# Small attentions: one row maximum and one clamp for two units, where each unit had its own

## The chip, the cores and the metric

The kernel runs on one core of a Trainium2 chip. The metric is the device time of one execution in microseconds; where several executions are given, the median is meant. A core has TensorE (PE, matrix products and transposes), VectorE (DVE), ScalarE (ACT), GpSimd (POOL) and a queue that starts DMAs (SP). Each engine works through its own list of instructions strictly in the order in which the program wrote them; between engines, order comes from semaphores alone: an instruction waits until a counter has reached a value, and counts another one up when it ends.

## The reference

Thirty-two sequences of 128 tokens with 128 features (`x`) go through four layers, each a cross attention to a context of the same size and then a feed-forward part; every part reads a layer-normalised `x` and is added back to it with a gate `tanh(g)`. The parts differ: layer 0 is a 16-head attention with a mask and a mixture of experts, layer 1 a 16-head attention and an attention whose value and output projections are switched by a router, layer 2 an mLSTM and a convolution, layer 3 a one-head attention and another mixture of experts. What matters here are the two "small" attentions, those of layers 0 and 1:

```python
score = einsum('bhqd,bhkd->bhqk', qh, kh) / sqrt(8)      # 16 heads of 8 features, 128 x 128 scores each
score = where(mask == 0, -inf, score)                    # layer 0; layer 1: where(mask, score, -1e9)
attn  = softmax(score, axis=-1)                          # exp(score - max) / sum
out   = einsum('bhqk,bhkd->bhqd', attn, v) @ w_o + b_o
```

All arithmetic is in float32. The row maximum only keeps the exponentials in range; the clamp of layer 0 keeps a row that is masked throughout away from infinity.

## The kernel before, in words

**Tiling.** The 32 sequences are done in 8 turns. In a turn two lanes (`k` = 0 and 1) work side by side, each on G = 2 sequences, and each lane goes through the eight stages A0 (small attention of layer 0), M0, A1 (small attention of layer 1), SW, ML, CF, WA, M3. The lanes share the engines, and each lane has four of the eight PSUM banks: `banks[2k]` is one tensor of 1024 columns that covers its banks 0 and 1, `banks[2k+1]` its banks 2 and 3. `bank(k, n)` is one of them, 512 float32 columns.

**Order.** Every engine's work is written as a generator for each lane that yields between chunks. `weave` merges the two generators of an engine by tables of due times, `BEATS_PE`, `BEATS_ACT`, `BEATS_DVE`; the result is a fixed order of chunks, the same in every turn, in which chunks of lane 0 and lane 1 alternate. `SPARES` is a table of extra products of TensorE whose results nobody reads (L336). The change touches neither tables nor yields.

**A small attention** (`pe_small_attention`, `act_small_attention`, `dve_small_attention`) has 2 sequences x 16 heads = 32 score maps, in 8 units of 4 heads. Two units make a pair:

1. TensorE, `scores(p)`: for each of the pair's two units the mask is put into bank 0 (even unit) or bank 1 (odd unit), L383, and then the product of queries and keys is added to it, L386. The next pair's masks wait for `p_ok` of both units of this one.
2. VectorE, `dve_max` (L1202, called at L1238): the negated row maximum of the four maps of a unit, 128 x 512 in, 128 x 4 out, into the tile `nm`; in A0 a clamp of these four columns follows (L1206). Counts up `nm_ok`.
3. ScalarE, `act_map`: waits for `nm_ok` of its unit and makes four exponentials, L862, into `P`. Counts up `p_ok`.
4. TensorE, `pe_turn_map`: waits for `p_ok` of its unit and for the copy of the unit before, and makes four transposes into bank 2, L450.
5. VectorE copies them to `PT`, L1245 (`pT_ok`).
6. TensorE, `values(u)`: the product with the values, L397. After four units the outputs are turned (L408), and VectorE divides them by the row sums (`dve_small_out`, L1258 and L1260).

In VectorE's list of one lane the chunks are: maximum of the even unit, maximum of the odd unit, copy, copy, and again. Between the two maxima `weave` may put chunks of the other lane, and in each turn it does so for 10 of the 16 pairs. `dve_max` also serves SW and WA, which the change leaves as they are.

Of the kernel before, what the change touches and what calls it, by code (L numbers as in the profile page):

```python
# [11 lines left out]
ALU = mybir.AluOpType  # L12
ACT = mybir.ActivationFunctionType
AX = mybir.AxisListType
# [7 lines left out]
HQ = 4  # L22
NEG = -1.0e30
# [180 lines left out]
def b3(ap, n=G):  # L204
    return ap.rearrange("p (b c) -> p b c", b=n)
# [9 lines left out]
def cols(n, width=128):  # L215
    return slice(n * width, (n + 1) * width)


def build(nc, x_in, ctx_in, ctxT_in, mask0_in, mask1_in, w_in, pick_in, out):
    with ExitStack() as ctx:  # L220
# [3 lines left out]
        def pair(name, cols, dt=F32):  # L224
            return [sb(f"{name}_{k}", cols, dt) for k in range(LANES)]

        def sem(name):
            return ctx.enter_context(nc.semaphore(name))

        def signal(name, per):  # L230
            return Signal([sem(f"{name}_{k}") for k in range(LANES)], per)
# [10 lines left out]
        s_ps, nm_ok, p_ok = signal("s_ps", 25), signal("nm_ok", 25), signal("p_ok", 25)  # L242
# [16 lines left out]
        vt, at, = Ticks([sem(f"dve_step_{k}") for k in range(LANES)]), Ticks([sem(f"act_step_{k}") for k in range(LANES)])  # L259

        banks = [ctx.enter_context(nc.psum_tensor(f"banks{i}", [128, 1024], F32)) for i in range(4)]
# [42 lines left out]
        nm = pair("nm", 16)  # L304
# [15 lines left out]
        def bank(k, n):  # L320
            return banks[2 * k + n // 2][:, cols(n % 2, 512)]
# [781 lines left out]
        def dve_layernorm(dve, k, i, j, src, dst, sig):  # L1103
            s3, d3 = b3(src[:, :]), b3(dst[:, :])
            st3, mv3 = st[k][:, :].rearrange("p (b c) -> p b c", b=G), mv[k][:, :].rearrange("p (b c) -> p b c", c=2)
            for b in range(G):
                dve.bn_stats(st3[:, b, :], s3[:, b, :]).then_inc(vt.up(k), 1)
            dve.wait_ge(vt[k], vt.n[k])
            for b in range(G):
                dve.bn_aggr(mv3[:, b, :], st3[:, b, :]).then_inc(vt.up(k), 1)  # L1110
            yield from dve_rstd(dve, k, i, j, mv3[:, :, 1], 1.0, LN_EPS)
            dve.wait_ge(vt[k], vt.n[k])
            for b in range(G):
                e = dve.tensor_scalar(d3[:, b, :], s3[:, b, :], mv3[:, b, 0:1], mv3[:, b, 1:2], ALU.subtract, ALU.mult)  # L1114
            e.then_inc(sig, 1)
# [21 lines left out]
        def dve_gated_add(dve, k, i, stage, y, n):  # L1137
            dve.wait_ge(y_ps[k], y_ps.n(i, y))
            layer = stage // 2 + 4 * (stage % 2)
            dve.scalar_tensor_tensor(x[i % 2][k][:, :], bank(k, n)[:, 0:T], tg[:, layer:layer + 1], x[i % 2][k][:, :],  # L1140
                                     ALU.mult, ALU.add).then_inc(x_up[k], 1)
# [56 lines left out]
        def dve_max(dve, k, i, n, first, scores, maps, clamp):  # L1198

            m = nm[k][:, first:first + maps]  # L1200
            dve.wait_ge(s_ps[k], s_ps.n(i, n))
            e = dve.tensor_reduce(m, b3(scores[:, 0:maps * 128], maps), AX.X, ALU.max, negate=True)  # L1202
            if clamp:
                e.then_inc(vt.up(k), 1)
                dve.wait_ge(vt[k], vt.n[k])
                e = dve.tensor_scalar(m, m, -NEG / 10, None, ALU.min)  # L1206
            e.then_inc(nm_ok[k], 1)

        def dve_small_attention(dve, k, i, s):
            stage = (A0, A1)[s]  # L1210
            ln = dve_layernorm(dve, k, i, (VE_A0, VE_A1)[s], x[i % 2][k], xn[k], xn_ok[k])
            yield
            if s == 0:
                if i == 0 and k == 0:
                    dve.wait_ge(s_gates, 1)
                dve.wait_ge(x_ld[k], 16 * (i + 1))
                dve.wait_ge(ctx_ld[k], 48 * (i + 1))
                if i:
                    dve.wait_ge(x_up[k], x_up.n(i - 1, M3))
                dve.tensor_scalar(mb0[k][:, :], m_ld[k][:, :], 0.0, NEG, ALU.is_equal, ALU.mult)  # L1220
            else:
                dve.wait_ge(x_up[k], x_up.n(i, stage - 1))
            next(ln)
            v4 = va[k][:, 0:G * H * 32].rearrange("p (b h d) -> p b h d", b=G, h=H)
            if s == 0:
                dve.memset(va[k][:, 0:G * H * 32], 0.0).then_inc(vt.up(k), 1)
                dve.wait_ge(vt[k], vt.n[k])
                dve.memset(v4[:, :, :, DH], 1.0)
            yield
            dve.wait_ge(v_ps[k], v_ps.n(i, s))  # L1230
            dve.tensor_copy(v4[:, :, :, 0:DH].rearrange("p b h d -> p (b h) d"),
                            bank(k, 1)[:, 0:T].rearrange("p (n d) -> p n d", d=DH)).then_inc(v_ok[k], 1)
            yield
            next(ln, None)
            late = dve_constants(dve) if i + k + s == 0 else iter(())
            for u in range(8):
                yield
                dve_max(dve, k, i, 8 * s + u, 4 * (u % 4), bank(k, u % 2), HQ, s == 0)  # L1238
                if u % 2:
                    for n in (u - 1, u):  # L1240
                        yield
                        dve.wait_ge(pT_ps[k], pT_ps.n(i, 8 * s + n))
                        if n >= 2:
                            dve.wait_ge(o_ps[k], o_ps.n(i, 8 * s + n - 2))
                        dve.tensor_copy(PT[k][:, cols(n % 2, 512)], bank(k, 2)).then_inc(pT_ok[k], 1)  # L1245
                next(late, None)
            yield
            dve_small_out(dve, k, i, s, 0)
            yield
            dve_small_out(dve, k, i, s, 1)  # L1250
            yield
            dve_gated_add(dve, k, i, stage, (Y_A0, Y_A1)[s], 1)

        def dve_small_out(dve, k, i, s, b):
            rec = sm[k][:, cols(b, H)]
            o3 = bank(k, 2 * b).rearrange("p (h d) -> p h d", h=H)
            dve.wait_ge(ot_ps[k], ot_ps.n(i, 2 * s + b))
            dve.reciprocal(rec, o3[:, :, DH]).then_inc(vt.up(k), 1)  # L1258
            dve.wait_ge(vt[k], vt.n[k])
            dve.tensor_tensor(oa[k][:, cols(b)].rearrange("p (h d) -> p h d", h=H), o3[:, :, 0:DH], bc(rec, 2, DH),  # L1260
                              ALU.mult).then_inc(o_ok[k], 1)
# [393 lines left out]
        def dve_constants(dve):  # L1655

            part = mixd[0][:, 0:256].bitcast(BF16)
            rest = w("rows")
            dve.wait_ge(s_w1, 48)
            dve.tensor_copy(part, rest).then_inc(s_rows, 1)  # L1660
            dve.tensor_copy(causb[:, :], w("causal"))
            yield
            for m in range(3):
                pick = w("part3", m, m + 1)
                dve.wait_ge(s_rows, 3 * m + 1)
                if m == 0:
                    dve.tensor_scalar(rowsb[:, :], part, pick, None, ALU.mult).then_inc(s_rows, 1)
                else:
                    dve.scalar_tensor_tensor(rowsb[:, :], part, pick, rowsb[:, :], ALU.mult, ALU.add).then_inc(s_rows, 1)
                if m < 2:  # L1670
                    dve.wait_ge(s_rows, 3 * m + 2)
                    dve.tensor_tensor(rest, rest, part, ALU.subtract).then_inc(s_rows, 1)
                    yield
                    dve.wait_ge(s_rows, 3 * m + 3)
                    dve.tensor_copy(part, rest).then_inc(s_rows, 1)
            yield
            dve.tensor_copy(pick3b[:, :], pick_ld)
            dve.tensor_copy(pick0b[:, :], w("pick0"))
            yield
            dve.tensor_scalar(mb1[:, :], m1_ld[:, :], 0.0, NEG, ALU.is_equal, ALU.mult)  # L1680
            dve.tensor_scalar(bq1s[:, 0:1], w("bq1"), DH ** -0.5, None, ALU.mult)
            for j in range(HQ):
                e = dve.tensor_tensor(bkm[:, j:j + 1], w("bk1"), w("head4", j, j + 1), ALU.mult)
            e.then_inc(s_rows, 1)
# [247 lines left out]
```

## Time and profile before

| | |
|---|---|
| median of 3 runs | 2445.72 us (2435.81 to 2452.79) |
| profiled execution | 2447.47 us, span of its instructions 2445.4 us |
| TensorE busy | 2223.2 us (91%) |
| VectorE busy | 1749.4 us (72%), 5567 instructions |
| ScalarE busy | 1290.7 us (53%) |
| GpSimd busy | 141.2 us (6%) |
| mean granted TensorE clock | 0.976 |
| chain that ended last | TensorE 49%, VectorE 30%, ScalarE 8%, DMA 5%, issue 4% |

Busy is time in which an engine executes, idle is time in which it waits. Since every engine goes by its list, the idle time of one that is at work almost always (TensorE) is what a change can give or take. The chain is followed back from the last instruction; TensorE's share of it says that for about half of the span it was TensorE's own work that came last.

### The profile page before, as it was taken

Reading aid. Unit: us, or ns where it says so; the run is one execution under the profiler, and the core shown is the slowest. Engines: PE = TensorE matmul, PEld = TensorE weight load, DVE = VectorE, ACT = ScalarE, POOL = GpSimd, SP = SyncE. Lnnn points to the kernel's source line nnn. Section 1 sums busy time; section 2 is a strip of 40 time slices with the busy share of each in tenths; the row PEclk is TensorE's granted clock in tenths of the full one; section 3 lists DMA queues with packets and bytes.
Section 4 is the critical chain, followed back from the end, with each engine's and each line's share of the span. In section 5 each row is a group of like instructions: output and inputs, shape, how many; then the busy total and the mean of one; then the engine's idle time right before and its main releaser. Section 6 shows DMA issues by size and latency. Waiting matters only on the chain.

```text
span 2445.4 us, 51545 instructions
## 1 busy us (share of the span) xinstructions
PE 2223.2 (91%) x19938; PEld 1612.2 (66%) x19938; DVE 1749.4 (72%) x5567; ACT 1290.7 (53%) x3714; POOL 141.2 (6%) x180
## 2 busy tenths in 40 slices
PE   7899989989899998999899988999889998899998
PEld 3668657676567765677666766667666676666766
DVE  6874787757877577774877758777587775877657
ACT  4366354664547545474444744547344473445734
POOL 0000100001000010000100010000110001100010
PEclk9999999999999899998999999999899998999989
DMA  4034000340004300042000520006100061000610
GB/s 172 1 88 104 9 14 1 96 96 10 14 1 113 79 9 14 1 122 70 9 14 1 129 63 9 14 1 147 45 18 6 2 156 36 20 3 13 151 29 5
DMA packets 312516, 115.52 MB, mean 47 GB/s; under 512 B 268752, under 2 KB 295376, under 8 KB 312016
## 3 DMA queue, kind: packets, MB, share of 16 engines
q1 hardware_dynamic: 312272, 112.23, 17.9%
q8 instruction: 158, 2.59, 0.4%
q14 instruction: 86, 0.70, 0.1%
HBM read 63.96 MB, written 48.23 MB: 46 GB/s over the span
## 4 chain that ended last, share of the span: by engine, by line
PE 49%; DVE 30%; ACT 8%; DMA 5%; issue 4%; POOL 3%; SPq 1%; DVEq 0%; ACTq 0%
PE banks L450 7%; PE banks L386 6%; PE banks L589 3%; PE banks L505 3%; ACT PP L862 3%; PE banks L616 3%; PE banks L383 2%; PE banks L336 2%; DVE nm L1202 2%; DVE qk L1283 2%; DMA mix_d<-gs 2%; PE banks L544 2%; PE banks L397 2%; PE banks L559 2%; POOL mv L1741 2%
## 5 line engine op out<-in xcount | busy, mean ns | idle before, releaser
L862 ACT ACTIVATE PP<-banks,nm 128x128 f32<-128x128 f32 x1568 | 443.7, 391 | 210.8 <-DVE nm L1202 120.5
L1202 DVE TENSOR_REDUCE nm<-banks 128x4 f32<-128x512 f32 (+1 forms) x400 | 261.3, 675 | 136.3 <-PE banks L386 100.7
L336 PE MATMUL banks<-identb 128*128 128x256 bf16 x1840 | 289.1, 277 | 16.4 <-ACT PP L1017 8.5
L450 PE MATMUL banks<-w_sb,PP 128*128 128x128 f32 x1536 | 247.8, 285 | 45.7 <-ACT PP L862 17.6
L450 PEld LDWEIGHTS banks<-w_sb,PP 128*128 128x128 f32 x1536 | 167.4, 142 | 122.9 <-issue 64.0
L336 PEld LDWEIGHTS banks<-identb 128*128 128x128 bf16 x1840 | 177.2, 101 | 106.6 <-issue 48.0
L1741 POOL TENSOR_TENSOR mv<-mv,half 128x2 f32<-128x2 f32 x160 | 113.0, 706 | 2135.0 <-DVE mv L1099 2135.0
L1245 DVE COPY PP<-banks 128x512 f32<-128x512 f32 x256 | 175.8, 689 | 61.1 <-PE banks L450 60.2
L505 PE MATMUL banks<-w_sb,qk 128*128 128x128 f32 x1280 | 180.6, 280 | 2.0 <-DVE qk L1346 1.3
L505 PEld LDWEIGHTS banks<-w_sb,qk 128*128 128x128 f32 x1280 | 164.7, 194 | 20.1 <-issue 11.4
L386 PE MATMUL banks<-qk,gs 32*128 32x512 f32 x512 | 147.5, 653 | 0.0
L589 PE MATMUL banks<-va,PP 128*128 128x128 f32 x1024 | 139.3, 282 | 2.3 <-DVE oa L1391 2.3
L589 PEld LDWEIGHTS banks<-va,PP 128*128 128x128 f32 x1024 | 124.6, 194 | 8.5 <-DVE oa L1391 4.2
L853 ACT ACTIVATE xnT<-banks 128x256 f32<-128x256 f32 x128 | 49.1, 384 | 149.0 <-PE banks L344 149.0
L544 PE MATMUL banks<-xnT,w_sb 128*128 128x256 f32 x512 | 121.0, 384 | 0.6
L916 ACT ACTIVATE tmp<-banks 128x256 f32<-128x256 f32 x160 | 60.5, 383 | 103.1 <-PE banks L475 102.3
L544 PEld LDWEIGHTS banks<-xnT,w_sb 128*128 128x128 f32 x512 | 94.0, 190 | 25.4 <-issue 7.7
L397 PE MATMUL banks<-PP,va 128*32 128x128 f32 x2048 | 102.8, 284 | 3.9 <-DVE PP L1245 3.9
L1346 DVE TENSOR_TENSOR qk<-qk,banks 128x256 f32<-128x256 f32 x256 | 96.2, 416 | 8.2 <-PE banks L498 4.4
L1114 DVE TENSOR_SCALAR xn<-x,mv 128x128 f32<-128x128 f32 x256 | 76.7, 342 | 34.0 <-POOL mv L1741 32.6
L474 PE MATMUL banks<-xnT,w_sb 128*128 128x256 f32 x320 | 97.9, 388 | 0.5 <-DVE wstat L1700 0.5
L475 PE MATMUL banks<-xnT,w_sb 128*128 128x256 f32 x320 | 95.6, 381 | 0.0
(283 smaller groups left out, 4267.4 us busy)
## 6 DMA issues: line engine op xcount, KB each, us to landing
va<-v_d SPq DMA_DIRECT2D x32, 512.0 KB, 3.8
o_d<-oa SPq DMA_DIRECT2D x64, 256.0 KB, 4.2
va<-o_d SPq DMA_DIRECT2D x32, 512.0 KB, 4.4
pv_d<-PP SPq DMA_DIRECT2D x32, 256.0 KB, 2.0
oa<-pv_d SPq DMA_DIRECT2D x32, 256.0 KB, 3.2
v_d<-PP SPq DMA_DIRECT2D x16, 512.0 KB, 4.0
v_d<-tmp SPq DMA_DIRECT2D x16, 512.0 KB, 4.4
w_sb<-weights SPq DMA_DIRECT2D x1, 5599.0 KB, 24.2
```

Source lines behind the costliest of these rows:

```text
L336: pe.matmul(bank(k, n)[:, cols(c, T)], identb[:, :], bc(identb[:, :], 1, G), start=True, stop=True, skip_group_check=True)
L386: pe.matmul(bank(k, c), qT[k][rows, cols(b)], km[rows, b, :], start=False, stop=True, skip_group_check=True).then_inc(s_ps[k], 1)
L397: e = pe.matmul(bank(k, 3)[32 * j:32 * j + 32, cols(g)], v4[:, b, HQ * g + j, :], PT[k][:, 512 * (u % 2) + 128 * j:][:, 0:128], start=True ...
L450: e = pe.transpose(bank(k, 2)[:, cols(j)], P[k][:, 512 * (u % 2) + 128 * j:][:, 0:128], ident)
L474: pe.matmul(hb[:, 0:T], w("w1_0", n * 128, (n + 1) * 128), xnT[k][:, :], start=True, stop=True)
L505: e = pe.matmul(bank(k, 0)[:, cols(b)], qk[k][:, n * T + b * 128:n * T + (b + 1) * 128], w(weight, n * 128, (n + 1) * 128), start=n == 8 a ...
L544: pe.matmul(bank(k, n % 4)[:, 0:T], w(("sq1", "sk1")[n % 2], n // 2 * 128, (n // 2 + 1) * 128), xnT[k][:, :], start=True, stop=True).then_ ...
L589: e = pe.matmul(bank(k, 3)[:, cols(j)], PT[k][:, 512 * (u % 2) + 128 * j:][:, 0:128], va3[k][:, n:G * H + 1:G * H - n, :], start=True, sto ...
L862: e = act.activation(P[k][:, 512 * (u % 2) + 128 * j:][:, 0:128], bank_[:, cols(j)], ACT.Exp, bias=nm[k][:, m:m + 1])
L1202: e = dve.tensor_reduce(m, b3(scores[:, 0:maps * 128], maps), AX.X, ALU.max, negate=True)
L1245: dve.tensor_copy(PT[k][:, cols(n % 2, 512)], bank(k, 2)).then_inc(pT_ok[k], 1)
L1741: pool.tensor_tensor(a, a, half[:, 0:n], ALU.pow).then_inc(pw[k], 1)
```

## The change

`dve_small_attention` no longer calls `dve_max` for each unit. In the chunk of an even unit nothing is left; in the chunk of the odd unit `dve_max_pair` takes the maxima of both units in one instruction over both banks (128 x 1024 in, 128 x 8 out), clamps the eight columns once in A0, and counts `nm_ok` up by 2. Over the kernel 256 reductions of 512 columns become 128 of 1024, and 128 clamps become 64. ScalarE's and TensorE's waits keep their values, so the exponentials of an even unit now wait for the pair's instruction.

```diff
+        def dve_max_pair(dve, k, i, n, first, clamp):
+
+            m = nm[k][:, first:first + 2 * HQ]
+            dve.wait_ge(s_ps[k], s_ps.n(i, n))
+            e = dve.tensor_reduce(m, b3(banks[2 * k][:, :], 2 * HQ), AX.X, ALU.max, negate=True)
+            if clamp:
+                e.then_inc(vt.up(k), 1)
+                dve.wait_ge(vt[k], vt.n[k])
+                e = dve.tensor_scalar(m, m, -NEG / 10, None, ALU.min)
+            e.then_inc(nm_ok[k], 2)
+
...
             for u in range(8):
                 yield
-                dve_max(dve, k, i, 8 * s + u, 4 * (u % 4), bank(k, u % 2), HQ, s == 0)
                 if u % 2:
+                    dve_max_pair(dve, k, i, 8 * s + u, 4 * (u % 4) - 4, s == 0)
                     for n in (u - 1, u):
                         yield
                         dve.wait_ge(pT_ps[k], pT_ps.n(i, 8 * s + n))
```

## Rows read from the trace of the kernel before

**Rows 1.** Page, part 1: busy time, share of the span, instructions.

```profile
PE 2223.2 (91%) x19938; PEld 1612.2 (66%) x19938; DVE 1749.4 (72%) x5567; ACT 1290.7 (53%) x3714; POOL 141.2 (6%) x180
```

**Rows 2.** Groups of VectorE by form: count | busy us, mean ns | idle before, releasers.

```profile
L1202 DVE TENSOR_REDUCE nm<-banks 128x4 f32<-128x512 f32 x384 | 254.6, 686 | 136.3 <-PE banks L386 100.7 <-PE banks L559 34.1
...
L1206 DVE TENSOR_SCALAR nm<-nm 128x4 f32<-128x4 f32 x128 | 21.8, 170 | 4.4
...
L1202 DVE TENSOR_REDUCE nm<-banks 128x2 f32<-128x256 f32 x16 | 6.7, 418 | 0.0
```

**Rows 3.** Timeline of VectorE, A1 of turn 2: start us, length us, what [idle before].

```profile
723.39 0.69 DVE L1202 TENSOR_REDUCE nm<-banks 128x4 f32<-128x512 f32 x1 [0.54 <-PE banks L386]
724.00 0.68 DVE L1245 COPY PP<-banks 128x512 f32<-128x512 f32 x1
725.43 0.69 DVE L1245 COPY PP<-banks 128x512 f32<-128x512 f32 x1 [0.75 <-PE banks L450]
726.91 1.29 DVE L1202 TENSOR_REDUCE nm<-banks 128x4 f32<-128x512 f32 x2 [0.79 <-PE banks L386]
728.12 0.68 DVE L1245 COPY PP<-banks 128x512 f32<-128x512 f32 x1
...
732.71 0.68 DVE L1245 COPY PP<-banks 128x512 f32<-128x512 f32 x1
...
742.03 0.26 DVE L1258 RECIPROCAL sm<-banks 128x16 f32<-128x16 f32 x1
...
742.53 0.68 DVE L1202 TENSOR_REDUCE nm<-banks 128x4 f32<-128x512 f32 x1
```

**Rows 4.** Timeline of ScalarE, the same stage.

```profile
724.12 1.15 ACT L862 ACTIVATE PP<-banks,nm 128x128 f32<-128x128 f32 x4 [0.25 <-DVE nm L1202]
727.63 3.21 ACT L862 ACTIVATE PP<-banks,nm 128x128 f32<-128x128 f32 x12 [2.37 <-DVE nm L1202]
```

**Rows 5.** Timeline of TensorE, the same stage; the last rows from narrow windows.

```profile
718.81 0.63 PE L450 MATMUL banks<-w_sb,PP 128*128 128x128 f32 x4 [0.50 <-ACT PP L862]
...
722.23 1.13 PE L386 MATMUL banks<-qk,gs 32*128 32x512 f32 x4
723.29 0.66 PE L450 MATMUL banks<-w_sb,PP 128*128 128x128 f32 x4
...
726.81 0.66 PE L450 MATMUL banks<-w_sb,PP 128*128 128x128 f32 x4
...
728.92 0.63 PE L450 MATMUL banks<-w_sb,PP 128*128 128x128 f32 x4 [0.88 <-ACT PP L862]
...
734.44 0.66 PE L450 MATMUL banks<-w_sb,PP 128*128 128x128 f32 x4
...
743.27 0.63 PE L450 MATMUL banks<-w_sb,PP 128*128 128x128 f32 x4 [0.17 <-ACT PP L862]
```

**Rows 6.** Timeline of VectorE, A0 of turn 2.

```profile
633.99 0.69 DVE L1202 TENSOR_REDUCE nm<-banks 128x4 f32<-128x512 f32 x1 [1.06 <-PE banks L386]
...
649.91 0.68 DVE L1245 COPY PP<-banks 128x512 f32<-128x512 f32 x1
...
660.72 0.69 DVE L1245 COPY PP<-banks 128x512 f32<-128x512 f32 x1
```

**Rows 7.** Timeline of ScalarE, A0 of turn 2.

```profile
634.92 2.18 ACT L862 ACTIVATE PP<-banks,nm 128x128 f32<-128x128 f32 x8 [2.69 <-DVE nm L1206]
```

**Rows 8.** Timeline of TensorE, A0 of turn 2, in narrow windows.

```profile
651.32 0.30 PE L450 MATMUL banks<-w_sb,PP 128*128 128x128 f32 x1
...
662.41 0.66 PE L450 MATMUL banks<-w_sb,PP 128*128 128x128 f32 x4
...
668.40 0.63 PE L450 MATMUL banks<-w_sb,PP 128*128 128x128 f32 x4 [0.15 <-ACT PP L862]
```

**Rows 9.** Windows of two turns: length, busy of PE PEld DVE ACT POOL, granted clock, DMA.

```profile
1236.09:1534.80 298.71, 272.34 (x2493) 197.89 (x2493) 216.77 (x690) 161.07 (x464) 17.62 (x22) 0.99 0.18 44
1534.80:1838.07 303.27, 277.47 (x2494) 202.19 (x2493) 216.81 (x690) 161.16 (x464) 17.62 (x22) 0.97 0.18 44
```

## The prediction

> **What bounds the kernel now.** The page's first part comes first: TensorE is busy for 91% of the span, VectorE for 72%, ScalarE for 53% [rows 1]. So the time is TensorE's list of instructions plus the holes in it, and a change on VectorE counts only where it makes a hole of TensorE's wider or narrower. A turn of 298.71 us has 272.34 us of TensorE in it, so 26 us of holes [rows 9]. The timelines of one small attention on VectorE, ScalarE and TensorE tell which step ends a hole: TensorE stands before a unit's transposes (L450) for its exponentials, 0.50 us at 718.81, 0.88 us at 728.92, 0.17 us at 743.27 [rows 5], and the exponentials stand for the maximum [rows 4]. From the first maximum of a pair to the transposes of its even unit there is hardly slack in these places. That is where the change acts. The pattern is the same, to a few hundredths of a microsecond, in turns 1 to 7, and nearly so in A1 of turn 0; I work it out for turn 2.
>
> **What does not change.** All four products of a pair (two units) run as one group, 1.13 us from 722.23, to 723.36, and the even unit's maximum starts at 723.39 [rows 5, 3]. It does not start while the odd unit's products run, so waiting for both units costs nothing at this point.
>
> **The instruction itself.** 512 columns take 686 ns, 256 take 418 ns [rows 2]: 1.047 ns a column, so 1024 columns would take 686 + 512 x 1.047 = 1222 ns, an estimate from these two. Bounds: without any fixed part 1024 x 1.047 = 1.07 us; as two old ones, 1.37 us. I take 1.22, since the two forms are the same operation on the same memory. VectorE is relieved: in A1 by 2 x 0.686 - 1.22 = 0.15 us a pair, in A0, where one clamp of 0.170 goes too, by 0.32 us; with 64 pairs each 9.6 + 20.5 = 30 us of busy time. This is off the path except where TensorE waits for VectorE itself.
>
> **The even unit gets its maximum later.** Before, its exponentials start 0.73 us after the maximum starts (723.39 to 724.12), in A0 0.93 us (633.99 to 634.92), 0.20 us more for the clamp [rows 3, 4, 6, 7]. With the pair they start after 1.22 + 0.04 = 1.26 us, in A0 after 1.46 us. The exponentials take 1.14 us and the transposes follow 0.14 us later (727.63 + 1.15 + 0.14 = 728.92) [rows 4, 5]. So from the start of the pair's maximum to the transposes it is **2.54 us in A1, 2.74 us in A0**. The delay of 0.53 us is the small part.
>
> **The even unit loses its place in the queue.** The pair's instruction stands where the odd unit's stood. For 10 of the 16 pairs of a turn work of the other lane stands between the two, and the pair now waits for it. In A1 of lane 0 the even maximum runs at 723.39, then come two copies of lane 1 at 724.00 and 725.43, the second of which waits 0.75 us for TensorE, and only after lane 1's even maximum, in the middle of the row of two at 726.91, lane 0's odd one [rows 3]. In the new list lane 0 has no maximum before 725.43 + 0.61.
>
> Followed along TensorE's list through A1 (each later place starts from the shift reached so far):
> 1. Lane 0's second pair: its maximum starts about 716.90, its transposes at 719.44 instead of 718.81 [rows 5]: **+0.63**.
> 2. Lane 1's first pair: its products are 0.63 late, its maximum starts at 721.59, transposes 724.13 instead of 723.29: **+0.84**.
> 3. Lane 0's third pair: the copy at 725.43 goes to 726.27, the maximum follows after 0.61 us as at 723.39 to 724.00, so 726.88, transposes 729.42 instead of 726.81: **+2.61**.
> 4. Lane 1's second pair is behind lane 0's copy (728.12), and that copy now waits for the transposes just named: they end 0.66 us later, at 730.08, the copy starts at 730.11, the maximum at 730.72, transposes 733.26 instead of 728.92: **+4.34**. ScalarE's list has lane 1's exponentials of this unit ahead of lane 0's odd ones (the x12 of 727.63, three units), so lane 0's next transposes wait behind them as well.
> 5. Lane 0's fourth pair is behind lane 1's copy at 732.71, now 737.05; maximum 737.66, transposes 740.20 instead of 734.44: **+5.76**, of which TensorE's own small holes up to the next place give back 0.14.
> 6. Lane 1's last pair is behind the divisions of lane 0 at 742.03, now 747.65; its maximum follows after 0.50 us as at 742.53, so 748.15, transposes 750.69 instead of 743.27: **+7.4**.
>
> A0 in the same way, with 2.74 us and less VectorE time for the clamps:
> 1. The first pairs of both lanes add 0.6, and 0.2 come back where a copy no longer stands behind an even maximum; lane 1's units 0 and 1 bring it to 0.67.
> 2. Lane 0's third pair is behind lane 1's copy of 649.91, now 650.57; maximum 651.18, transposes 653.92 instead of 651.32: **+2.60**.
> 3. Two pairs add 0.24 (2.84). Lane 1's third pair is behind lane 0's copy of 660.72, now 663.56; maximum 664.17, transposes 666.91 instead of 662.41: **+4.50** [rows 6, 8].
> 4. Lane 1's last pair is behind lane 0's divisions as in A1, transposes some 674.6 instead of 668.40: **+6.2**.
>
> What is late next is everything: the last transposes stand in TensorE's list ahead of the output projection of lane 0, so the residual, the next layer norm and all later stages start with the shift. Nothing outside the attentions is loaded late enough by DMA to swallow it. Per turn 7.4 + 6.2 = 13.6 us, in 8 turns **109 us**.
>
> **The clock.** The list gets seven new holes a turn of 1.4 to 2.6 us. Turns at different granted clock differ in time for the same work: 298.71 us at 0.99, 303.27 us at 0.97 [rows 9], 4.6 us. Bounds for what the holes bring: 0, and one such step in each turn, 37 us. I take a quarter, 9 us, because a turn with 26 us of holes in it ran at 0.99 of the 2.4 GHz.
>
> **The sum.** 2447.5 (the profiled execution; 1.8 us above the median of the three runs) + 109 + 9 = **2565 us**, 4.9% slower.
>
> **Rivals.**
> - **A, VectorE's relief counts and the path hides the rest** (faster side). Place: the copies and maxima that TensorE waits for, and A0's clamps. Price: at most the 30 us above, 2417 us; half of it 2432. For it: the chain of waits gives 30% of the span to VectorE. Against it: TensorE's holes before transposes end with exponentials, not with VectorE. It decides if, in the places counted above, the transposes had 2 us of slack or more. The Trainium skill has a rule on this side, "VectorE: DVE Perf Modes", section "Rules for kernel authors": of chained VectorE operations, keep the number low. By that rule, the 192 instructions less would be a gain of up to these 30 us; the trace agrees on the busy time, but VectorE is not what fills the span. Chance 0.05.
> - **B, only the longer instruction counts** (place in the queue doesn't matter, as the other lane's work is ready early enough). Then a place costs 0.53 us; about 7 places a turn have no slack, so 3.7 us a turn, 30 us, 2477 us. For it: 6 pairs have nothing between. Against it: the copy at 725.43 itself waited for TensorE. Chance 0.09; with slack in half of these places 2462 us, within 1% of before, 0.05 more.
> - **C, the clock falls oftener**. One step from 0.99 to 0.97 in each turn and the whole shift: 2447.5 + 109 + 37 = 2593 us; two steps a turn 2630 us. For it: TensorE idles 2.6 us where it idled 0.88. Against it: turns with holes of their own at 0.99. The Trainium skill, "TensorE: Matmul & The Clock Gate", section "Part 1: The HAM clock gate", says that an idle TensorE goes to half rate, 1.2 GHz; by that, the seven holes are the risk. Chance 0.16.
> - **D, the change doesn't do what it says**: the reduction across two banks takes longer than 1.37 us, say 1.6. About 14 maxima of a turn are on the path; 0.38 x 14 x 8 = 43 us more, 2608 us. Nothing in the trace speaks for it. Chance 0.03.
>
> **The numbers.** The forecast, all of the shift with little clock, has 0.62. Its own range: 1.07 to 1.37 us for the maximum on 14 places in 8 turns is 17 us either way, the first turn's A0 (different work between) 6 us, and slips of the count some 20 us, so 2525 to 2600. The range over all reaches into C, **2515 to 2610 us**; outside are A, B and the far end of C and D. About 1% of the time, 24 us, is what a measurement can tell from no change. Faster by more: that part of A near its full price, 0.03. Within: the rest of A and the weak form of B, 0.07. Slower: 0.90.
>
> **What would show it.** VectorE's maxima: 128 of 128 x 1024 near 1.22 us, and VectorE's busy time down by some 30 us, in every case. For the forecast: TensorE's idle time up by about 110 us, nearly all of it before L450 and ended by L862; the third pair of lane 0 in A1 with its maximum some 2.7 us after its products instead of at once; turns of some 313 us; 7 us in A1 and 6 us in A0, and nothing in M0, ML, CF, WA, M3. For B: turns of 302 us. For C: a mean clock under 0.96. For A: turns under 298 us. I would be wrong if the transposes in the places above didn't move by the steps given, most of all steps 3 and 4 of A1.

## The result, and the profile after

The changed kernel takes 2633.64 us (median of 4 runs, 2626.35 to 2639.82), the kernel before 2445.97 us: the ratio is 1.0763 with a 95% interval of 1.073 to 1.0797. It is 188 us slower, where 2565 us, 119 us more, was forecast, in a range of 2515 to 2610 us. The sign was right; the time lies 24 us above the range.

The page of the changed kernel, first busy time and then the costliest groups that the change touches (line, engine, operation, form, count | busy us, mean ns | idle before, releaser):

```profile
PE 2324.9 (88%) x19938; PEld 1662.2 (63%) x19938; DVE 1729.1 (66%) x5375; ACT 1284.8 (49%) x3714; POOL 141.0 (5%) x180
...
L862 ACT ACTIVATE PP<-banks,nm 128x128 f32<-128x128 f32 x1568 | 440.0, 392 | 384.7 <-DVE nm L1217 181.1
L450 PE MATMUL banks<-w_sb,PP 128*128 128x128 f32 x1536 | 279.9, 311 | 138.9 <-ACT PP L862 116.2
...
L1213 DVE TENSOR_REDUCE nm<-banks 128x8 f32<-128x1024 f32 x128 | 155.5, 1217 | 49.9 <-PE banks L386 49.3
```

Against [rows 1] TensorE is busy for 102 us more, with the same 19938 products and transposes, and idle for 87 us more. So there are more holes, and the same work takes longer. Idle time before the transposes (L450) that the exponentials (L862) end is 116.2 us; in the trace of the kernel before it is 17.6 us. VectorE has 20 us less to do. The new maximum takes 1217 ns, against 1222 ns estimated from [rows 2].

The third and second pairs of A1, VectorE of the changed kernel, for [rows 3] (start us, length us):

```profile
778.18 0.69 DVE L1256 COPY PP<-banks 128x512 f32<-128x512 f32 x1 [0.75 <-PE banks L450]
778.79 1.21 DVE L1213 TENSOR_REDUCE nm<-banks 128x8 f32<-128x1024 f32 x1
781.99 0.69 DVE L1256 COPY PP<-banks 128x512 f32<-128x512 f32 x1 [1.99 <-PE banks L450]
782.60 1.21 DVE L1213 TENSOR_REDUCE nm<-banks 128x8 f32<-128x1024 f32 x1
```

ScalarE and TensorE of the same stretch, for [rows 4, 5]:

```profile
780.04 1.14 ACT L862 ACTIVATE PP<-banks,nm 128x128 f32<-128x128 f32 x4 [3.01 <-DVE nm L1213]
783.85 3.20 ACT L862 ACTIVATE PP<-banks,nm 128x128 f32<-128x128 f32 x12 [2.67 <-DVE nm L1213]
```

```profile
778.51 1.13 PE L386 MATMUL banks<-qk,gs 32*128 32x512 f32 x4
781.33 0.63 PE L450 MATMUL banks<-w_sb,PP 128*128 128x128 f32 x4 [1.69 <-ACT PP L862]
781.88 0.64 PE L397 MATMUL banks<-PP,va 128*32 128x128 f32 x16
785.13 1.09 PE L450 MATMUL banks<-w_sb,PP 128*128 128x128 f32 x4 [2.60 <-ACT PP L862]
...
788.64 2.08 PE L386 MATMUL banks<-qk,gs 32*128 32x512 f32 x4
...
792.54 2.08 PE L386 MATMUL banks<-qk,gs 32*128 32x512 f32 x4
```

This is to be seen: lane 0's maximum starts at 778.79 behind lane 1's copy, its transposes at 781.33, which is 2.54 us later. Those set lane 0's copy free (781.99), which lets lane 1's maximum start (782.60), and 2.53 us later lane 1's transposes run, at 785.13, after a hole of 2.60 us. The two holes of before were 0 and 0.88 us [rows 5]. Up to here it is the forecast step by step. But behind the hole the same instructions take twice as long: four transposes 1.09 us instead of 0.63, four score products 2.08 us instead of 1.13.

The granted clock of the two attentions of that turn and of the rest; then the stretches behind a hole in A0 and behind the hole of 2.60 us in A1 (length, busy of PE PEld DVE ACT POOL, clock, DMA):

```profile
668.00:726.00 58.00, 48.60 (x347) 27.51 (x345) 31.81 (x69) 24.47 (x82) 1.41 (x3) 0.85 0.04 11
726.00:766.00 40.00, 38.45 (x243) 32.14 (x243) 33.55 (x116) 14.10 (x41) 1.39 (x2) 1.00 0.00 1
766.00:812.00 46.00, 38.28 (x274) 19.61 (x273) 23.59 (x45) 19.95 (x68) 1.39 (x2) 0.81 0.00 1
812.00:967.00 155.00, 140.67 (x1484) 110.00 (x1482) 98.80 (x331) 85.66 (x230) 10.61 (x12) 0.96 0.32 76
```

```profile
693.30:706.90 13.60, 13.59 (x66) 6.01 (x66) 6.02 (x9) 4.90 (x19) 0.00 (x0) 0.54 0.01 1
785.13:798.80 13.67, 13.67 (x76) 6.58 (x76) 5.18 (x7) 6.32 (x25) 0.00 (x0) 0.53 0.00 0
```

And the kernel before with the same 66 products and transposes of A0:

```profile
651.32:659.43 8.11, 7.90 (x66) 3.73 (x66) 6.54 (x14) 5.89 (x21) 0.00 (x0) 1.00 0.01 2
```

TensorE works without a hole for 13.6 us at 0.54 of its clock (1.2 GHz in nearly all of it) for what before took 8.1 us at 2.4 GHz. That is 5.5 us in one turn's A0, and A1 has a stretch like it. Not every turn has both: in the changed kernel's trace A1 has one interval of 13.7 to 17.1 us at 1.2 GHz in turns 0, 2, 5 and 7, and of only 6.8 us in turns 1, 3, 4 and 6, with the same instructions in the same order.

"Half clock" below is time at 1.2 GHz. The profiled executions can be compared from the second turn on: there it is 92 us before and 324 us after. Over the whole spans it is 116 and 396 us, but the clock's record of the kernel before starts only 36.5 us into the span. The four score products take 2.08 us there, which is their length at half clock, and the changed kernel's trace has 24 us of half clock up to that time; about as much (an estimate) is missing in the 116:

```profile
24.64 2.08 PE L386 MATMUL banks<-qk,gs 32*128 32x512 f32 x4
```

The 117 us of the expectations below is that whole-span number.

### The profile page after: what moved, and what is told of

It is laid out like the page before. It is cut to its first block, busy times and chain, and to the rows that moved or that the text cites. A ratio compares the mean times of both kernels' runs of the same rounds, so it can differ in the third digit from the quotient of the medians.

```text
span 2634.1 us, 51481 instructions
## 1 busy us (share of the span) xinstructions
PE 2324.9 (88%) x19938; PEld 1662.2 (63%) x19938; DVE 1729.1 (66%) x5375; ACT 1284.8 (49%) x3714; POOL 141.0 (5%) x180
## 3 DMA queue, kind: packets, MB, share of 16 engines
q8 instruction: 158, 2.59, 0.4%
## 4 chain that ended last, share of the span: by engine, by line
PE 45%; DVE 31%; ACT 9%; DMA 5%; issue 5%; POOL 3%; SPq 1%; DVEq 0%; ACTq 0%
PE banks L450 8%; PE banks L386 5%; ACT PP L862 4%; DVE nm L1213 4%; PE banks L589 3%; PE banks L397 3%; PE banks L336 3%; PE banks L616 2%; DVE qk L1294 2%; DMA mix_d<-gs 2%; PE banks L383 2%; PE banks L505 2%; DVE tmp L1292 2%; POOL mv L1752 2%; PE banks L722 2%
## 5 line engine op out<-in xcount | busy, mean ns | idle before, releaser
L862 ACT ACTIVATE PP<-banks,nm 128x128 f32<-128x128 f32 x1568 | 440.0, 392 | 384.7 <-DVE nm L1217 181.1
L450 PE MATMUL banks<-w_sb,PP 128*128 128x128 f32 x1536 | 279.9, 311 | 138.9 <-ACT PP L862 116.2
L450 PEld LDWEIGHTS banks<-w_sb,PP 128*128 128x128 f32 x1536 | 186.4, 155 | 232.9 <-issue 166.5
L336 PE MATMUL banks<-identb 128*128 128x256 bf16 x1840 | 292.3, 279 | 13.6 <-ACT PP L1017 7.3
L1213 DVE TENSOR_REDUCE nm<-banks 128x8 f32<-128x1024 f32 x128 | 155.5, 1217 | 49.9 <-PE banks L386 49.3
L505 PEld LDWEIGHTS banks<-w_sb,qk 128*128 128x128 f32 x1280 | 168.9, 198 | 20.5 <-issue 11.4
L386 PE MATMUL banks<-qk,gs 32*128 32x512 f32 x512 | 169.3, 742 | 0.0
L397 PE MATMUL banks<-PP,va 128*32 128x128 f32 x2048 | 120.6, 327 | 1.6 <-DVE PP L1256 1.5
L544 PE MATMUL banks<-xnT,w_sb 128*128 128x256 f32 x512 | 120.9, 384 | 0.5
L1202 DVE TENSOR_REDUCE nm<-banks 128x4 f32<-128x512 f32 x144 | 89.6, 654 | 36.6 <-PE banks L559 36.3
L397 PEld LDWEIGHTS banks<-PP,va 128*32 128x32 f32 x2048 | 47.9, 120 | 86.0 <-issue 69.0
```

The source lines that it names most:

```text
L336: pe.matmul(bank(k, n)[:, cols(c, T)], identb[:, :], bc(identb[:, :], 1, G), start=True, stop=True, skip_group_check=True)
L386: pe.matmul(bank(k, c), qT[k][rows, cols(b)], km[rows, b, :], start=False, stop=True, skip_group_check=True).then_inc(s_ps[k], 1)
L397: e = pe.matmul(bank(k, 3)[32 * j:32 * j + 32, cols(g)], v4[:, b, HQ * g + j, :], PT[k][:, 512 * (u % 2) + 128 * j:][:, 0:128], start=True ...
L450: e = pe.transpose(bank(k, 2)[:, cols(j)], P[k][:, 512 * (u % 2) + 128 * j:][:, 0:128], ident)
L505: e = pe.matmul(bank(k, 0)[:, cols(b)], qk[k][:, n * T + b * 128:n * T + (b + 1) * 128], w(weight, n * 128, (n + 1) * 128), start=n == 8 a ...
L544: pe.matmul(bank(k, n % 4)[:, 0:T], w(("sq1", "sk1")[n % 2], n // 2 * 128, (n // 2 + 1) * 128), xnT[k][:, :], start=True, stop=True).then_ ...
```

## The experiments

The theories at this point: (1) the place in VectorE's list makes the shift, about 13.6 us a turn, and half clock that follows the holes makes the rest of the 188 us; (2) the longer instruction, or its read across two banks, makes the loss wherever it stands; (3) half clock costs nothing more, since it lies where TensorE waits anyway, and the list makes it all.

**The pair in the even unit's place.**

```diff
-                if u % 2:
-                    dve_max_pair(dve, k, i, 8 * s + u, 4 * (u % 4) - 4, s == 0)
+                if u % 2 == 0:
+                    dve_max_pair(dve, k, i, 8 * s + u + 1, 4 * (u % 4), s == 0)
+                if u % 2:
```

> The pair's maximum (one instruction over both banks, one clamp) stands where the even unit's stood, ahead of the other lane's work, and waits for the odd unit's products. Theory 1 (the place in VectorE's list makes the shift, 13.6 us a turn; the half clock that follows makes the rest of the 188 us): only the 0.53 us of the longer instruction are left, in some 7 places a turn, and some are given back by VectorE's relief: 2445 to 2480 us, mean clock 0.965 to 0.98, VectorE's maxima at 1.22 us as in the changed kernel. Theory 2 (the length of the instruction, or the read across two banks, makes the loss, wherever it stands): 2580 us or more, clock 0.93 to 0.95.

Measured: 2513.41 us, ratio 1.0287 (1.0225 to 1.0349), clock 0.965. Moving the instruction forward gives back 120 of the 188 us, so theory 2 is out. But it is 33 us above theory 1's range: the length is not as harmless as I had it. In the trace the waits of TensorE are longer by 0.1 to 0.67 us in some eighteen places, one after the other; the place of step 4:

```profile
749.51 0.65 PE L450 MATMUL banks<-w_sb,PP 128*128 128x128 f32 x4
750.10 0.64 PE L397 MATMUL banks<-PP,va 128*32 128x128 f32 x16
752.27 0.63 PE L450 MATMUL banks<-w_sb,PP 128*128 128x128 f32 x4 [1.53 <-ACT PP L862]
```

The hole is 1.53 us where it was 0.88 us before [rows 5]. Followed through turn 2, TensorE's list loses 3.8 us in A0 and 3.3 us in A1 against the kernel before, not 3.7 us in all. Little of it is the clock: half clock from the second turn on is 120 us, against 92 us.

**Two maxima in the odd unit's place** (the kernel before, edited).

```diff
-                dve_max(dve, k, i, 8 * s + u, 4 * (u % 4), bank(k, u % 2), HQ, s == 0)
                 if u % 2:
+                    for m in (u - 1, u):
+                        dve_max(dve, k, i, 8 * s + m, 4 * (m % 4), bank(k, m % 2), HQ, s == 0)
```

> Both units keep their own maximum and clamp of 512 columns, but the even one stands in the odd unit's place, just ahead of the odd one: the place alone, without the longer instruction. Theory 1: the even unit's exponentials start 0.53 us earlier than in the changed kernel on each of some 14 maxima of a turn that follow one another, so 13.6 - 14 x 0.53 = 6.2 us a turn and 50 us in all by the list, and half clock on top: 2500 to 2590 us, mean clock 0.94 to 0.97. Theory 2: as before the change, 2440 to 2455 us.

Measured: 2559.46 us, ratio 1.0441 (1.0401 to 1.0482), clock 0.945. The place alone, without any longer instruction, loses 111 us, as theory 1 has it; half clock from the second turn on is 208 us. Its holes are those of the changed kernel, each about half a microsecond shorter:

```profile
763.94 0.63 PE L450 MATMUL banks<-w_sb,PP 128*128 128x128 f32 x4 [1.16 <-ACT PP L862]
764.50 0.65 PE L397 MATMUL banks<-PP,va 128*32 128x128 f32 x16
767.21 0.63 PE L450 MATMUL banks<-w_sb,PP 128*128 128x128 f32 x4 [2.07 <-ACT PP L862]
```

1.16 and 2.07 us, against 1.69 and 2.60 us after the change.

**The changed kernel with its holes filled.** In front of seven waits of a turn TensorE gets products that nobody reads, into the bank that the transposes will overwrite.

```diff
+HOLES = {(0, 0, 4): 16, (0, 1, 4): 14, (0, 1, 6): 16, (8, 0, 4): 14, (8, 1, 2): 22, (8, 0, 6): 11, (8, 1, 6): 16}
...
             spare(pe, k, 2)
+            for _ in range(HOLES.get((first, k, u), 0)):
+                pe.matmul(bank(k, 2)[:, 0:T], identb[:, :], bc(identb[:, :], 1, G), start=True, stop=True,
+                          skip_group_check=True)
             pe.wait_ge(p_ok[k], p_ok.n(i, first + u))
```

> The changed kernel, with 11 to 22 extra products of TensorE that nobody reads (256 columns, 0.11 us each) put into the seven widest new holes of a turn, just ahead of the transposes that wait; the order of everything else and VectorE's work stay. Theory 1, by its two parts (109 us of shift by the list, some 80 us by half clock): the half clock goes and the shift stays, 2545 to 2580 us, mean clock 0.96 to 0.98. Rival (theory 3: half clock is only where TensorE waits anyway and costs nothing more, the list makes all 188 us): 2625 to 2645 us at a high clock.

Measured: 2553.5 us, ratio 1.043 (1.0398 to 1.0461), clock 0.97. This run separates the clock from the list: TensorE does 872 products more and the kernel is 80 us faster than the changed one. The same place as above, in its trace:

```profile
760.93 1.13 PE L388 MATMUL banks<-qk,gs 32*128 32x512 f32 x4
761.99 1.70 PE L451 MATMUL banks<-identb 128*128 128x256 bf16 x14
763.65 0.66 PE L455 MATMUL banks<-w_sb,PP 128*128 128x128 f32 x4
764.24 0.64 PE L399 MATMUL banks<-PP,va 128*32 128x128 f32 x16
764.82 2.58 PE L451 MATMUL banks<-identb 128*128 128x256 bf16 x22
767.40 0.66 PE L455 MATMUL banks<-w_sb,PP 128*128 128x128 f32 x4
```

The transposes come at the same distances as without the filling, 2.72 and 3.75 us apart, against 2.82 and 3.80 us; the shift stays. But both groups now take 0.66 us, at full clock, where the second took 1.09 us. Turn 2 as a whole (before, after, after with filled holes):

```profile
632.83:933.96 301.13, 275.99 (x2493) 200.06 (x2493) 216.92 (x691) 161.06 (x464) 17.62 (x22) 0.98 0.18 44
```

```profile
671.97:1001.42 329.45, 292.51 (x2493) 209.17 (x2493) 214.59 (x667) 160.43 (x464) 17.60 (x22) 0.92 0.17 40
```

```profile
660.62:973.03 312.41, 287.12 (x2602) 209.42 (x2601) 214.24 (x667) 160.66 (x464) 17.61 (x22) 0.98 0.17 42
```

301.1, 329.5 and 312.4 us. Over the five turns from the third on the mean length is 301.3 us before, 326.3 us after and 314.4 us with filled holes, so 13.1 us a turn are the list's, of which the forecast had 13.6, and 11.9 us are the clock's, of which it had 1.1. The clock is rightly called held: half clock in these five turns is 68 us before, 236 us after and 68 us with filled holes.

**The kernel before without its spare products** (`for _ in range(next(spares[k]))` becomes `range(0)`).

> The kernel before, without any of its spare products (L336); the order of the rest stays, and the maxima are those of before. It measures the price of the clock where VectorE's list is untouched. Theory 1: TensorE falls to half clock in the stages with small holes, half-clock time goes from 117 us to 250 us or more, and the time rises by some 0.3 us for each microsecond of it: 2480 to 2560 us, although 1840 products fewer run. Theory 3: the time stays or falls, 2420 to 2450 us.

Measured: 2511.96 us, ratio 1.0246 (1.0217 to 1.0275), clock 0.922. As theory 1 said: 1840 products fewer, nothing else changed, and 64 us more. From the second turn on the profiled execution is 51 us longer and has 287 us of half clock instead of 92 us, so 0.26 us for each microsecond of it. (From the kernel with filled holes to the changed one it is 79 us for 222 us, 0.36 us for each.) Theory 3 is out.

**Two maxima in the even unit's place.**

```diff
-                dve_max(dve, k, i, 8 * s + u, 4 * (u % 4), bank(k, u % 2), HQ, s == 0)
+                if u % 2 == 0:
+                    for m in (u, u + 1):
+                        dve_max(dve, k, i, 8 * s + m, 4 * (m % 4), bank(k, m % 2), HQ, s == 0)
```

> Both units keep their own maximum and clamp; both stand in the even unit's place. With the kernel before, the changed one and the two runs of a pair in the even place and of two maxima in the odd place it closes the table of place and length. Theory 1 (place and length each cost, each about what it adds from a pair's products to the transposes, and half clock follows the holes): the even unit loses nothing, the odd one comes earlier, only the other lane's copy is behind by 0.6 to 0.8 us where it stood between: 2435 to 2475 us, clock 0.97 to 0.98. Rival (two maxima in a row and the copies behind them hurt by themselves, wherever they stand): 2510 us or more, as the pair in the even place.

Measured: 2496.6 us, ratio 1.0205 (1.0181 to 1.0229), clock 0.96. It lies between both expectations, 22 us above theory 1's and 13 us below the rival's, so it is a miss for both. I had counted what a pair's own exponentials gain and not what the other lane loses. Now the copies of the other lane stand behind two maxima, and TensorE waits for them (two views of the same stretch, VectorE and TensorE):

```profile
658.67 0.69 DVE L1202 TENSOR_REDUCE nm<-banks 128x4 f32<-128x512 f32 x1 [0.79 <-PE banks L386]
659.40 0.17 DVE L1206 TENSOR_SCALAR nm<-nm 128x4 f32<-128x4 f32 x1
659.48 0.68 DVE L1202 TENSOR_REDUCE nm<-banks 128x4 f32<-128x512 f32 x1
660.19 0.17 DVE L1206 TENSOR_SCALAR nm<-nm 128x4 f32<-128x4 f32 x1
660.27 0.68 DVE L1247 COPY PP<-banks 128x512 f32<-128x512 f32 x1
```

```profile
661.01 1.09 PE L450 MATMUL banks<-w_sb,PP 128*128 128x128 f32 x8 [1.36 <-DVE PP L1247]
```

The hole of 1.36 us was 0.57 us before: the copy, next in line at 649.91 [rows 6], comes after 1.60 us here and came after 0.81 us there. The place matters to whoever stands behind, also where no instruction is longer and no VectorE work is added. In turn 2 TensorE's list loses 4 us up to the end of A1, of some 6 us a turn. Half clock from the second turn on is 143 us; where the rest of the loss arises was not followed.

**Two maxima in the odd place, holes filled.** Six holes, 9 to 18 products each, inserted as above.

> Two single maxima in the odd place as in the earlier run, with 9 to 18 extra products of TensorE that nobody reads in the six widest new holes of a turn. Theory 1: the shift by the list alone, 6.5 to 7.5 us a turn, stays and half clock goes: 2495 to 2520 us at a clock of 0.96 to 0.98, against 2559 us without them. Theory 3 (half clock costs nothing): 2550 to 2570 us.

Measured: 2507.92 us, ratio 1.0239 (1.0202 to 1.0276), clock 0.973; 52 us faster than without the filling. Half clock from the second turn on is 113 us instead of 208 us. Place alone at nearly held clock: 61 us, 7.6 us a turn.

**The kernel before with two of its own holes filled**: 17 spare products in front of the gates of M3 (lane 0), 12 in front of the first column sums of ML (lane 1).

> The kernel before with its own two widest holes filled in each turn: 17 unread products before the gates of M3 in lane 0 (hole of 2.31 us), 12 before the first column sums of ML in lane 1 (1.58 us). Theory 1 says that half clock costs 0.3 us for each of its microseconds: if the 117 us of half clock fall to 60 us or less, 2425 to 2440 us; if they stay, since what stands before and behind these holes is light work too, 2440 to 2455 us. Theory 3: 2440 to 2455 us in either case.

Measured: 2440.19 us (10 runs), ratio 0.998 (0.9965 to 0.9995), clock 0.98. It is the only version that is not slower than before, and by 0.2% only. From the second turn on half clock is 58 instead of 92 us. At the 0.3 us of theory 1 these 34 us would be worth 10 us; the measured gain is 7 us, with an interval of 1 to 9 us. That is too small a step to tell the theories apart, and the price may be lower here.

**A pair only where nothing stands between** (6 of 16 pairs of a turn; VectorE's order is that of before).

```diff
+                if (s, k, u // 2) not in ((0, 0, 0), (0, 0, 1), (0, 1, 1), (1, 0, 0), (1, 0, 1), (1, 1, 0)):
                     dve_max(dve, k, i, 8 * s + u, 4 * (u % 4), bank(k, u % 2), HQ, s == 0)
+                elif u % 2:
+                    dve_max_pair(dve, k, i, 8 * s + u, 4 * (u % 4) - 4, s == 0)
                 if u % 2:
-                    dve_max_pair(dve, k, i, 8 * s + u, 4 * (u % 4) - 4, s == 0)
```

> One maximum for two units only in the 6 of 16 pairs of a turn where no work of the other lane stands between the two, so VectorE's order is that of before; the other 10 pairs keep two maxima. The length alone, where the place is no question. Theory 1: 0.5 to 0.65 us in the places without slack, 4 or 5 of the 6: 2.0 to 3.2 us a turn, 2460 to 2475 us, clock 0.965 to 0.975. Rival A of the prediction (relief of VectorE counts): 2430 to 2445 us.

Measured: 2470.5 us, ratio 1.0098 (1.0068 to 1.0128), clock 0.976. The length alone, with the clock nearly where it was (half clock from the second turn on 96 us, against 92): 24 us for 48 pairs, 0.49 us each. VectorE has 7 us less to do, and the kernel is slower all the same: rival A of the prediction fails where it had the best chance.

**The changed kernel with two of the seven holes filled**: `HOLES = {(0, 0, 4): 16, (8, 1, 2): 22}`.

> The changed kernel with only two of its seven widest new holes of a turn filled (16 unread products before the transposes of lane 0's unit 4 in A0, 22 before those of lane 1's unit 2 in A1); the other five, of 1.4 to 2 us, stay. In the changed kernel's trace these two holes of 2.0 and 2.6 us stand at the head of half clock of 13.65 us each, while the others go with 0 to 3.4 us. If the cost lies in the long stretches that begin at these two: 2555 to 2585 us, clock 0.955 to 0.97, most of what all seven gave (2553 us). If each hole costs about alike: 2 of 7 parts of the 82 us, 2600 to 2620 us, clock 0.93 to 0.945.

Measured: 2588.92 us, ratio 1.056 (1.0537 to 1.0584), clock 0.947 in the profiled run, which was the slowest of the five (2605.77 us). It lies between both expectations: these two holes had 45 of the 80 us, more than 2 of 7 parts and less than nearly all. So the other five count too, once these are gone. The trace shows more: in A1 of turns 1, 2 and 3 half clock now lasts 20.5 us, and it begins at a hole of 0.95 us that nobody filled, here in turn 2:

```profile
768.35 1.01 PE L455 MATMUL banks<-w_sb,PP 128*128 128x128 f32 x4 [0.95 <-ACT PP L867]
```

The changed kernel has the same hole of 0.95 us, at 771.34, and goes through it at 2.4 GHz. So neither the size of a hole nor its place in the list tells by itself whether half clock follows.

**The table**, difference to the kernel before, measured together with it (us), by place and length:

| | two of 512 | one of 1024 |
|---|---|---|
| each in its own place | 0 | - |
| even unit's place | +50 | +65 |
| odd unit's place | +111 | +188 |
| odd unit's place, holes filled | +61 | +105 |

With the holes filled, place alone is 61 us and the longer instruction in that place 44 us on top. With the clock left free the same step from two to one is 77 us.

## Why the prediction was right or wrong

**The instruction**, 1.22 us: measured 1.217 us. Right. VectorE's relief was 20 us of busy time, not 30: instructions in a row overlap in the trace (two maxima take 1.29 us, and a copy starts 0.61 us after a maximum of 0.69 us [rows 3]), and the sum of durations counts this twice. Nothing hung on it.

**The delay from a maximum to the transposes**, 2.54 us in A1: measured 781.33 - 778.79 = 2.54. In A0 2.74 us was forecast, and it is 2.81 us (690.50 to 693.31). Right.

**The places in the list.** How late TensorE is at each place of turn 2 against the kernel before, counted from the start of the attention, in us (with the filled holes the clock is held):

| place | forecast | changed kernel | holes filled |
|---|---|---|---|
| A0, step 2 | 2.60 | 2.85 | 2.75 |
| A0, step 3 | 4.50 | 10.06 | 4.79 |
| A0, step 4 | 6.2 | 11.78 | 6.45 |
| A1, step 1 | 0.63 | 0.70 | 0.70 |
| A1, step 2 | 0.84 | 0.93 | 0.93 |
| A1, step 3 | 2.61 | 2.69 | 2.59 |
| A1, step 4 | 4.34 | 4.38 | 4.23 |
| A1, step 5 | 5.76 | 8.87 | 5.63 |
| A1, step 6 | 7.4 | 11.75 | 7.11 |

Up to the first long hole of each attention the changed kernel goes as forecast, and behind it half clock is added. Its own growth at step 5 of A1 did not come there: TensorE is so slow at that place that VectorE and ScalarE catch up, and its transposes start at 795.14 without a wait. With filled holes all steps come. In each of the turns 1 to 7, A0 then costs 6.4 to 6.5 us and A1 7.1 us, and M0 costs nothing; in the changed kernel A0 costs 11.8 to 14.5 us and A1 8.9 to 13.2 us. With filled holes the turns are 13 us longer, as forecast, and the whole is +105 us against the 109 us of the sum. The mechanism and its size are right. That the whole came out so near is in part luck: the stages behind A1 give back up to 2.3 us in some turns and cost up to 2.6 us in others, where the forecast had nothing.

**The clock** is the step that failed: "I take a quarter, 9 us, because a turn with 26 us of holes in it ran at 0.99". It measured 80 us (2633.6 against 2553.5 with filled holes). The price of a given fall was right: [rows 9] give 4.6 us a turn for 0.02 of clock, and the turns from the third on lost 11.9 us for 0.05 (0.978 with filled holes, 0.928 without). What was mis-sized is the fall: I put it at a quarter of 0.02. Its upper bound, 37 us, failed too, because I had taken it from the difference between two turns of the kernel before (0.99 and 0.97), as if one more step of that size were the most that could come. The changed turn 2 has 0.92. What I had not seen is that a hole inside these attentions is not paid once: TensorE went to 1.2 GHz at it and could stay there for 13.6 us of work without a hole. The average of holes over a turn says nothing of that. Rival C had the mechanism, and by twice its step the size ("two steps a turn 2630 us"), with a chance of 0.16 over both forms. No row spoke for two steps rather than one or three, so that its number came so near is luck; and the range ended at 2610 us, between its first and its second step. Its sign, a mean clock under 0.96, came: 0.925.

The Trainium skill, "TensorE: Matmul & The Clock Gate", section "Part 1: The HAM clock gate", was cited for the risk that an idle TensorE falls to half rate. The traces agree on the two levels and on falls at holes, though not at every hole. The same section has the engine back at full rate after a short stretch of sustained work; here it was not back through 13.6 us in which the profile shows it busy for 13.59, so for this mix of transposes and small products the measurement decides.

**Rival A** (relief counts) is excluded by the run with six pairs, **rival B** (only the length) by the two maxima in the odd place, **rival D** (read across two banks) by the measured 1217 ns. What rival B stood for was itself mis-sized: the length alone costs 65 us in the even place, in some eighteen places a turn of 0.1 to 0.67 us, and not 30 us in seven of 0.53.

**What stays open**: why the clock stayed down through gapless work, and why the same instructions bring 6.8 us of half clock in one turn and 17.1 us in another. The work there is transposes of four, products of 32 rows (L386) and of 32 columns (L397), and the kernel before goes through the same work at 2.4 GHz. In turn 2 it does so when it arrives at full clock and not when it arrives at half; what the gate counts was not measured.

## What to carry to other kernels

When one instruction takes the work of two, look first at where it stands in the engine's list: it can start no earlier than its later half did, and what stood between the halves now stands before it; follow that through the lists of all engines, because each wait feeds the next. A saving on an engine that the bound engine doesn't wait for showed no gain here (VectorE had 20 us less to do in the changed kernel and 7 us less with six pairs, and both were slower). Don't price new holes in TensorE by their sum over a turn, nor by the clock of a kernel that lacks them: test the clock's share by filling them with unread products. Here 872 of these made a kernel 80 us faster.

## What the runs showed of the hardware that was not expected

TensorE stayed at 1.2 GHz in nearly all of 13.6 us of work in which it was busy for 13.59 us, behind a hole of 2.02 us, and the same work took 8.1 us at 2.4 GHz in the kernel before. A hole of 0.95 us stood at the head of 20.5 us of half clock in one kernel and of none in another. A microsecond at half clock cost 0.26 us in one pair of runs and 0.36 us in another, not a half or more; in the one place followed here (step 5 of A1) the other engines catch up meanwhile. The maximum of 1024 columns across two PSUM banks took 1217 ns; a straight line through 256 columns (418 ns) and 512 (686 ns) gives 1222 ns.
